# Attention with latent keys and values: the value and output weights on fp16 high/low parts with scales worked out on the chip, in place of float32r

## The reference

```python
xn = layernorm(x)
q = (xn @ wq)                 # 16 heads of 128 + 64 (rotary) columns
kva = xn @ wkv_a              # 128 latent + 64 rotary columns
ckv = rmsnorm(kva[:128]) * kv_norm_scale
kv = ckv @ wkv_b              # per head: 128 key columns, 128 value columns
scores = (q_nope . k_nope + rope(q_pe) . rope(k_pe)) * 192 ** -0.5
attn = softmax(causal(scores))
out = concat_heads(attn @ v) @ wo          # wo: 16 * 128 rows, 512 columns
ffn = sum over r of (xn @ factors[r]) / sqrt(8) + bias
return x + out + ffn
```

## Time and profile before

| | |
|---|---|
| median of 3 runs | 1571.4 us (1571.31 to 1575.96) |
| profiled execution | 1576.8 us, span of its trace 1574.7 us |
| busy in the span: TensorE, VectorE, ScalarE, GpSimd | 96%, 66%, 60%, 58% |
| TensorE instructions | 7876 |
| mean granted TensorE clock | 0.988 of full |
| the chain that ended last | TensorE 86%, VectorE 6%, ScalarE 4% |

### The profile page before, as it was taken

One profiled execution on the slowest core, in us unless ns is written; L12 is line 12 of the kernel. 1 busy time (PEld: TensorE's weight loads), 2 busy tenths in 40 slices (PEclk: granted clock), 3 DMA queues, 4 the chain that ended last, 5 costly groups with the idle time before them and its releaser, 6 DMA issues.

```text
span 1574.7 us, 25255 instructions
## 1 busy us (share of the span) xinstructions
PE 1514.0 (96%) x7876; PEld 819.7 (52%) x7876; DVE 1033.9 (66%) x2356; ACT 952.3 (60%) x2329; POOL 915.3 (58%) x897
## 2 busy tenths in 40 slices
PE   5669999999999999999999999999999999999998
PEld 4524555555555555455555555555555555555555
DVE  6755667666766665555555555556756776786887
ACT  6654766676666756556666666665546566554554
POOL 2665666566666666556656565656636655564553
PEclk9879999999999999999999999999999999999999
DMA  8635787878777789678777677787867667864564
GB/s 268 213 91 114 154 166 147 162 159 164 166 158 160 145 167 192 137 155 182 151 171 147 141 155 153 159 170 145 192 135 148 145 148 158 183 145 111 131 146 131
DMA packets 646883, 246.68 MB, mean 157 GB/s; under 512 B 599392, under 2 KB 612192, under 8 KB 646112
## 3 DMA queue, kind: packets, MB, share of 16 engines
q1 hardware_dynamic: 646752, 245.08, 72.3%
HBM read 79.30 MB, written 23.07 MB: 65 GB/s over the span
## 4 chain that ended last, share of the span: by engine, by line
PE 86%; DVE 6%; ACT 4%; issue 2%; POOL 1%; DMA 0%; SPq 0%; ACTq 0%; DVEq 0%; POOLq 0%
PE ps L356 17%; PE ps L358 17%; PE ps L357 17%; PE ps L491 7%; PE ps L496 7%; PE ps L497 7%; PE ps L492 7%; PE ps L493 7%; ACT ex L701 2%; DVE gm L1017 1%; DVE ps L1019 1%; DVE kt L966 1%; DVE acc L1062 0%; DVE nm L1035 0%; DVE stats L813 0%
## 5 line engine op out<-in xcount | busy, mean ns | idle before, releaser
L1218 POOL TENSOR_TENSOR st<-ex,st 128x512 f16<-128x512 f32 (+3 forms) x640 | 636.7, 1012 | 552.0 <-ACT st L711 540.6
L701 ACT ACTIVATE ex<-ps,nm,scales 128x512 f32<-128x512 f32 (+3 forms) x640 | 452.1, 709 | 542.5 <-DVE nm L1035 542.5
L1017 DVE TENSOR_REDUCE gm<-ps 128x1 f32<-128x512 f32 (+1 forms) x384 | 252.0, 669 | 209.7 <-PE ps L497 205.8
L711 ACT ACTIVATE st<-ex 128x512 f16<-128x512 f32 (+3 forms) x640 | 342.2, 561 | 6.1 <-ACT ex L701 0.4
L491 PE MATMUL ps<-kTh,q 128*128 128x512 f16 (+3 forms) x640 | 225.1, 352 | 5.5 <-DVE kRl L981 3.6
L496 PE MATMUL ps<-kRh,q 128*128 128x512 f16 (+3 forms) x640 | 223.4, 349 | 3.1 <-POOL q L1209 3.1
L492 PE MATMUL ps<-kTl,q 128*128 128x512 f16 (+3 forms) x640 | 223.8, 350 | 0.0
L493 PE MATMUL ps<-kTh,q 128*128 128x512 f16 (+3 forms) x640 | 223.7, 350 | 0.0
L497 PE MATMUL ps<-kRl,q 128*128 128x512 f16 (+3 forms) x640 | 223.4, 349 | 0.0
L356 PE MATMUL ps<-pT,vH 128*128 128x512 f16 (+3 forms) x640 | 223.2, 349 | 0.0
L357 PE MATMUL ps<-pT,vH 128*128 128x512 f16 (+3 forms) x640 | 222.2, 347 | 0.0
(11 more groups left out here) (187 smaller groups left out, 2282.7 us busy)
## 6 DMA issues: line engine op xcount, KB each, us to landing
wV<-w_vo SPq DMA_DIRECT2D x48, 512.0 KB, 3.7
wA<-w_abs SPq DMA_DIRECT2D x48, 256.0 KB, 3.0
pT<-st SPq DMA_TRANSPOSE x640, 3.2
early<-factors_in SPq DMA_DIRECT2D x32, 256.0 KB, 3.8
w_vo<-wV SPq DMA_DIRECT2D x16, 512.0 KB, 3.1
wP<-w_pe SPq DMA_DIRECT2D x24, 256.0 KB, 3.0
wsq<-wq_in SPq DMA_DIRECT2D x16, 256.0 KB, 3.5
wso<-wo_in SPq DMA_DIRECT2D x16, 256.0 KB, 2.9
```

What stands on the lines that cost most here:

```text
L701: e.activation(ex[:, n % NEX, 0:keys], s_bank(n)[:, 0:keys], ACT.Exp, bias=nm[:, (i * QT + r) % 4:(i * QT + r) % 4 + 1], scale=scales[:, p ...
L711: e.activation(stage(n, keys)[:, :, 0, :], ex[:, n % NEX, 0:keys].rearrange("p (t n) -> p t n", n=P), ACT.Copy).then_inc(z["a_pH"], 1)
L1017: e.tensor_reduce(m, b, AX_X, ALU.max).then_inc(z["v_max"], 1)
L1218: e.tensor_tensor(s[:, :, 1, :], ex[:, n % NEX, 0:keys].rearrange("p (t n) -> p t n", n=P), s[:, :, 0, :], ALU.subtract).then_inc(z["g_pL" ...
```

## The change

- `wX`, `wKV`, `wV` and `oT` become fp16 high and low parts. `wV` has a third slot, its high part divided by 2048, and the low part of `oT` is kept times 2048 (`LOW`), so the head output is three matmuls written out.
- Every head's value and output weight gets a scale: ScalarE squares and sums `wo` (`sqo`, 128x512, at r = 3) and the value weight (`sqv`, 128x128, at r = 0), TensorE sums both over the partitions ("nv", a 128x2 product with ones at r = 0), VectorE makes the scales (`scale_value`). 1/scale goes into `rden`.
- `w_o` moves from r = 0 to r = 1 (high part on ScalarE with the scale, low part from GpSimd to VectorE); "tkv" moves from r = 0 to r = 1, behind "tq"; "den" moves from r = 1 to r = 3 in the stage of chunk 3 and gets one more instruction everywhere.
- `read_output` gets one more ScalarE instruction, `oS` = high part times 2048, between the high part and VectorE's low part.
- In the prologue the transposes move from tiles 5 and 9 to 8 and 11, w_abs from 8 and 11 to 10 and 13. Storing and loading `w_vo` moves 384 KB in place of 512 KB.

```diff
@@ fills(i, r)
     if r == 0:
...
         if 1 <= i <= H:
-            out += [("wo", i - 1), ("wo_low", i - 1)]
+            out.append(("sqv", i - 1))
...
     if r == 0:
-        if i + 2 <= H + 2:
-            out.append(("tkv", i + 2))
+        if 1 <= i <= H:
+            out.append(("nv", i - 1))
...
         if i + 2 < H:
             out.append(("tq", i + 2))
-        if 1 <= i <= NU:
+        if i + 2 <= H + 2:
+            out.append(("tkv", i + 2))
+        if 1 <= i <= H:
+            out += [("wo", i - 1), ("wo_low", i - 1)]
+        if H <= i <= NU:
             out.append(("den", i - 1))
...
     if r == 3:
+        if 1 <= i < H:
+            out.append(("den", i - 1))
+        if 1 <= i <= H:
+            out.append(("ws", i - 1))
+        if i < H:
+            out.append(("sqo", i))
@@ buffers
-        wX = sb("wX", [P, 2, E], F32R)
-        wKV = sb("wKV", [P, 2, 2 * P], F32R)
+        wX = sb("wX", [P, 2, E], F16)
+        wKV = sb("wKV", [P, 2, 2 * P], F16)
-        wV = sb("wV", [P, 2, 2, E], F32R)
-        oT = sb("oT", [P, 2, CH], F32R)
+        wV = sb("wV", [P, 2, 3, E], F16)
+        oT = sb("oT", [P, 2, CH], F16)
@@ TensorE, head_output
+                    e.wait_ge(z["a_ws"], i + 1)
...
-                three(b, [oT[:, a, t * P:(t + 1) * P] for a in range(2)],
-                      [wV[:, i % 2, a, :] for a in range(2)]).then_inc(z["p_out"], 1)
+                o = [oT[:, a, t * P:(t + 1) * P] for a in range(2)]
+                e.matmul(b, o[0], wV[:, i % 2, 0, :], start=True, stop=False)
+                e.matmul(b, o[0], wV[:, i % 2, 1, :], start=False, stop=False)
+                e.matmul(b, o[1], wV[:, i % 2, 2, :], start=False, stop=True).then_inc(z["p_out"], 1)
+                elif kind == "nv":
+                    norm((kind, n), ("a_sqv", "a_sqo"), nv[:, :])
@@ ScalarE
+            def value_squares(kind, h):
...
+                e.activation(sqs[:, at:at + n], w, ACT.Square, accum_out=nv[:, at0:at0 + 1]).then_inc(
+                    z["a_" + kind], 1)
+
+            def w_vo_small(h):
+                e.wait_ge(z["v_wvo_hi"], h + 1)
+                e.activation(wV[:, h % 2, 2, :], wV[:, h % 2, 0, :], ACT.Copy, scale=1.0 / LOW).then_inc(z["a_ws"], 1)
@@ ScalarE, read_output
-                e.activation(oT[:, 0, :], ps[:, OB, :], ACT.Copy).then_inc(z["a_o"], 1)
+                e.activation(oT[:, 0, :], ps[:, OB, :], ACT.Copy, scale=shrink(chunk(i))).then_inc(z["a_o"], 1)
+                e.wait_ge(z["a_o"], i + 1)
+                e.activation(oS[:, :], oT[:, 0, :], ACT.Copy, scale=LOW).then_inc(z["a_oS"], 1)
@@ ScalarE, between the third and the fourth piece
-                                if kind in ("q", "wo", "parts"):
+                                if kind in ("q", "wo", "parts", "sqv"):
@@ VectorE
+            def scale_value(h):
...
+                e.wait_ge(z["p_nv"], h + 1)
+                e.tensor_tensor(t[:, 0:2], bank(("nv", h))[:, 0:2], tiny[:, :].broadcast_to([P, 2]), ALU.max).then_inc(
+                    z["v_nv"], 1)
+                e.wait_ge(z["v_nv"], h + 1)
+                root(t[:, 2:4], t[:, 0:2]).then_inc(z["v_vroot"], 1)
+                e.wait_ge(z["v_vroot"], h + 1)
+                e.tensor_tensor(t[:, 4:5], t[:, 2:3], t[:, 3:4], ALU.mult)
+                e.tensor_scalar(sc[:, 0:2], t[:, 2:4], WS, None, ALU.mult).then_inc(z["v_vw"], 1)
+                e.wait_ge(z["v_vw"], h + 1)
+                e.reciprocal(sc[:, 2:3], t[:, 4:5]).then_inc(z["v_vsc"], 1)
@@ VectorE, den
-                e.reciprocal(rden[:, i % 2, :], tsum[:, i % 2, :]).then_inc(z["v_den"], 1)
+                e.reciprocal(rtmp[:, i % 2, :], tsum[:, i % 2, :]).then_inc(z["v_rd"], 1)
+                e.wait_ge(z["v_rd"], i + 1)
+                if i < H:
+                    e.wait_ge(z["v_vsc"], i + 1)
+                e.scalar_tensor_tensor(out=rden[:, i % 2, :], in0=rtmp[:, i % 2, :], scalar=1.0 / (WS * shrink(c)),
+                                       in1=vsc[:, i % H, 2:3].broadcast_to([P, QT]), op0=ALU.mult,
+                                       op1=ALU.mult).then_inc(z["v_den"], 1)
@@ VectorE, read_output
-                e.wait_ge(z["a_o"], i + 1)
-                e.tensor_tensor(oT[:, 1, :], ps[:, OB, :], f(oT[:, 0, :]), ALU.subtract).then_inc(z["v_o"], 1)
+                e.wait_ge(z["a_oS"], i + 1)
+                e.scalar_tensor_tensor(out=oT[:, 1, :], in0=ps[:, OB, :], scalar=LOW * shrink(chunk(i)), in1=oS[:, :],
+                                       op0=ALU.mult, op1=ALU.subtract).then_inc(z["v_o"], 1)
```

More of the change, by code:

```diff
@@ L152, in fills @@
     return out
-IN_BANKS = ("q", "pe", "tkv", "wvo", "tq", "wabs", "out", "ffn", "nrm", "nf")
+IN_BANKS = ("q", "pe", "tkv", "wvo", "tq", "wabs", "out", "ffn", "nrm", "nf", "nv")
 def bank_order():
@@ L567, in _ @@
                 if t in (8, 11):
-                    w_abs(t // 3 - 2)
+                    wq_transpose(t // 3 - 2)
+                    kv_transpose(t // 3 - 2)
+                if t in (10, 13):
+                    w_abs(t // 3 - 3)
                 if t % 2 == 1 and 0 <= p - 2 < NP:
@@ L735, in fill @@
                     squares(kind, n)
+                elif kind in ("sqo", "sqv"):
+                    value_squares(kind, n)
+                elif kind == "ws":
+                    w_vo_small(n)
                 elif kind == "sqf":
@@ L803, in _ @@
                     for kind, n in fills(i, r):
-                        if last < 2 or r >= 2 or kind not in ("q", "wo", "parts"):
+                        if last < 2 or r >= 2 or kind not in ("q", "wo", "parts", "sqv"):
                             fill(kind, n)
@@ L900, in wq_transpose @@
                     e.wait_ge(z["p_wabs"], h)
-                e.tensor_copy(wX[:, 0, :], b).then_inc(z["v_tq_hi"], 1)
+                e.wait_ge(z["v_w2"], h // 2 + 1)
+                size = scales[:, h // 2, 0:1]
+                e.tensor_scalar(wX[:, 0, :], b, size, None, ALU.mult).then_inc(z["v_tq_hi"], 1)
                 e.wait_ge(z["v_tq_hi"], h + 1)
-                e.tensor_tensor(wX[:, 1, :], b, f(wX[:, 0, :]), ALU.subtract).then_inc(z["v_tq"], 1)
+                e.scalar_tensor_tensor(out=wX[:, 1, :], in0=b, scalar=size, in1=wX[:, 0, :], op0=ALU.mult,
+                                       op1=ALU.subtract).then_inc(z["v_tq"], 1)
             def kv_transpose(m):
-                cols = kv_cols(m)
-                b = bank(("tkv", m))[:, cols]
+                b = bank(("tkv", m))
+                parts = []
+                if m < H:
+                    e.wait_ge(z["v_w2"], m // 2 + 1)
+                    parts.append((slice(0, P), scales[:, m // 2, 1:2]))
+                if m >= 3:
+                    e.wait_ge(z["v_vw"], m - 2)
+                    parts.append((slice(P, 2 * P), vsc[:, m - 3, 0:1]))
                 e.wait_ge(z["p_tkv"], m + 1)
@@ L912, in kv_transpose @@
                     e.wait_ge(z["p_wvo"], m - 3)
-                e.tensor_copy(wKV[:, 0, cols], b).then_inc(z["v_tkv_hi"], 1)
+                for cols, size in parts:
+                    ins = e.tensor_scalar(wKV[:, 0, cols], b[:, cols], size, None, ALU.mult)
+                ins.then_inc(z["v_tkv_hi"], 1)
                 e.wait_ge(z["v_tkv_hi"], m + 1)
-                e.tensor_tensor(wKV[:, 1, cols], b, f(wKV[:, 0, cols]), ALU.subtract).then_inc(z["v_tkv"], 1)
+                for cols, size in parts:
+                    ins = e.scalar_tensor_tensor(out=wKV[:, 1, cols], in0=b[:, cols], scalar=size,
+                                                 in1=wKV[:, 0, cols], op0=ALU.mult, op1=ALU.subtract)
+                ins.then_inc(z["v_tkv"], 1)
             def w_abs(h):
@@ L1089, in fill @@
                     scale_pair(n)
+                elif kind == "nv":
+                    scale_value(n)
+                elif kind == "wo_low":
+                    w_o(n)
                 elif kind == "nf":
@@ L1249, in _ @@
                             scale_values(n)
-                        elif kind == "wo_low":
-                            w_o(n)
                         elif kind == "pe":
```

101 lines of the change are left out of this document (59 added, 42 removed).

## The result

The changed kernel takes 1630.1 us (median of 4 runs, 1627.1 to 1633.6), the kernel before 1571.6: 1.037 times as long, with an interval of 1.034 to 1.040. The forecast was 1627, in a range of 1596 to 1652.

What follows compares the result with a forecast made beforehand. TensorE was taken to bound chunks 3 to 1, a chain ScalarE, VectorE, TensorE chunk 0. Chunk 3's terms gave +54 us, the later stages and end +1.7; +55.7 on the median of 1571.4 made 1627, range 1596 to 1652.

Steps and rivals of the forecast that it cites:

- What bounds the kernel: TensorE decides in chunks 3 to 1, its waits paid in full; in chunk 0 a chain ScalarE, VectorE, TensorE.
- The wait of "nv": Chunk 3, r = 0: TensorE waits for sqv, queued behind q and exponentials on ScalarE; 42 us in sum.
- The clock: TensorE falls to 1.2 GHz behind long waits: nine of 2.5 us and more cost 15.3, those of 2.16 cost 5.
- "tkv" at r = 1: Even units: TensorE waits for the head output's bank, which VectorE reads; 0.7 us six times, 4 (bounds 0 to 15).
- The old waits before "nrm": TensorE's waits of 0.3 us in seven units go: minus 2.1 us.
- The cheaper matmuls: fp16 gains 0.08 us per head output, 20 over 256 if all count; w_abs and w_vo gain 9.5 in chunk 3.
- Chunks 2 and 1: Chunk 2: minus 4.8 us from matmuls; chunk 1: minus 1.8, as oS costs 3.0 there.
- Chunk 0: oS paid at 0.47 us in each of 16 heads, 7.6; den's instruction set against cheaper matmuls (bounds minus 4.8, plus 16).
- A: Rival: the waits come but the clock stays, or chunk 0 gains its matmuls in full; 1607 or 1592 us; chance 0.22.
- B: Rival: VectorE blocked by GpSimd at two-SBUF-input instructions in chunks 0 and 1; plus 15 to 20, 1645 us; chance 0.15.
- C: Rival: faster, "nv" finds its sums ready or TensorE's order does not bind; minus 28, 1543 us; chance 0.05.
- D: Rival: no change, waits of half the size and no clock effect nearly eaten by the gains; chance 0.03.

Runs made afterwards that it cites:

- Experiment 2: The changed kernel with 9 to 14 matmuls of 512 columns, their result overwritten, put on TensorE ahead of "nv"; 1615.6 us (1.026).
- experiment 1: The changed kernel with ScalarE's sqv ahead of the first exponential of r = 0 in place of behind q; 1604.9 us (1.021).
- experiment 4: The kernel before with only the fp16 high and low parts and fixed powers of two as scales, nothing moved; 1549.4 us (0.985).
- experiment 8: The kernel before with fp16 parts and fixed scales, plus oS as a copy on which VectorE's low part waits; 1558.5 us (0.991).
- experiment 9: The kernel before with fp16 parts and fixed scales, plus den's added instruction with a factor of one; 1551.5 us (0.987).
- experiment 6: The changed kernel with sqv ahead of the first exponential of r = 0 and "tkv" at r = 2, ahead of the values; 1598.6 us (1.017).
- experiment 7: The changed kernel with sqv ahead of r = 0's exponentials, "tkv" at r = 2, without oS, ws and wV's third slot; 1588.3 us (1.009).

## Why the prediction was right

**What bounds the kernel: right.** Waits in the stage of chunk 3 were paid in full. The stage lost 48.5 us where the sum had 54; of the 54, 5 belong to unit 1 (its wait 3.2, its product 0.2, its fall of the clock 1.7), which lies ahead of the cut, so like against like it is 49. That agreement is closer than its terms: the matmuls gained 11.1 there, not 13.7, and the clock took 16.2 more than before, not 18.6. The difference between the change and the types alone there, 562.5 - 502.9 = 59.5 us, is the sum of what the two profiles show: TensorE idle 42.7 against 5.6 (37.1), 84 against 8 slow matmuls (76 x 0.213 = 16.2), 15 products "nv" of 0.22 (3.3), and 0.165 for each of 15 more waits, because a printed wait begins at the end of a 0.38 us row while the next matmul would have started 0.215 behind its start (2.5). Together 59.1.

**The wait of "nv": right in place and size.** Forecast 42 us in sum; measured 42.5. Odd units 1.97 (2.16 forecast), even 3.15 (3.25; the first of them, unit 2, 3.62), units 1, 14 and 16 3.01, 2.53 and 3.25 (3.2, 2.6, 3.45). Three errors in single terms: `sqo` takes 0.61, not the 0.78 of an exponential of its size; 0.47, 0.47 and 0.78 are 1.72, not 1.74; and unit 15 was forecast with 0.3 on top of its old wait for q of 2.42, where "nv" took that wait's place with 2.53, so that the new waits net of the old one are 40, not 42.

**The clock: right in sum, by chance in its parts.** Forecast 20.3 us (15.3 and 5); 84 slow matmuls cost 17.9, of which 1.7 were there before. The rule "2.5 us and more falls, below half" did not hold unit by unit: the waits of 3.01 in unit 1 and 3.15 in unit 8 brought no fall, two of the six of 1.97 did, and the sum came near because these misses nearly cancel. Rows of the windows behind the wait in unit 4, in unit 8 and in unit 7, of 3.15, 3.15 and 1.97 us:

```profile
263.00:269.00 6.00, 5.40 (x20) 2.38 (x21) 3.64 (x11) 2.17 (x9) 2.50 (x3) 0.72 0.73 142
416.00:422.00 6.00, 5.42 (x31) 3.12 (x31) 5.36 (x17) 2.34 (x9) 2.10 (x3) 1.00 0.75 150
379.00:385.00 6.00, 6.00 (x25) 2.64 (x25) 3.11 (x10) 0.94 (x4) 1.67 (x3) 0.72 0.88 170
```

A fall cost 1.7 us (8 slow matmuls) in seven of its ten places, as the earlier trace rows had it. Experiment 2 shows that it is the standing still, and not the later start, that costs it.

**"tkv" at r = 1: right.** Forecast 0.7 in six units (4), measured 0.49 (2.9). The upper bound of 2.5, "if VectorE stayed as far behind", is what nearly came (2.36) when experiment 1 took the earlier wait away. The old waits before "nrm" (2.1 us) went, as forecast.

**The cheaper matmuls: right in kind, too large.** A head output gains 0.067 us in chunk 2 (4.26 over 64), not 0.08: the earlier trace rows are one place of 256, and the size was not checked against a second. By experiment 4 the types give 22 us, where the sum had 20 and 9.5.

**Chunks 2 and 1: -3.2 and -3.5 for -4.8 and -1.8.** The sum is right, the split is not. By experiment 8 oS costs 1.1 in chunk 2, 0.7 of it in one wait at its last heads; in chunk 1 the change is 0.8 over the types alone, where the forecast had 3.0 for oS: the slack of 0.1 in the earlier trace rows is that of one head.

**Chunk 0: right in sum, partly by chance.** Forecast +7.6, measured +9.0. That the chain through ScalarE pays for oS was right, its size was not: 0.47 in each of 16 heads was forecast, and what shows is 0.67 in each of nine waits, about one for a pair of heads, 6.0 by experiment 8. den costs 1.5 and the matmuls gain 2.7, which the sum had set equal. The falls of the clock, 2.8, were not in the sum for this stage, and 1.4 is without a cause.

**The rivals.** A (the clock stays) falls with the 84 slow matmuls and experiment 2. B (VectorE blocked by GpSimd at den, 15 to 20 us) falls with experiment 9, where den's instruction costs 1.5 us, all in chunk 0. Its rows in the changed kernel, and those of w_o's low part:

```profile
L1026 DVE SCALAR_TENSOR_TENSOR wV<-wso,vsc,wV 128x512 f16<-128x512 f32 x16 | 15.0, 935 | 15.6 <-ACT wV L711 15.6
L1136 DVE SCALAR_TENSOR_TENSOR rden<-rtmp,vsc 128x4 f32<-128x4 f32 x64 | 11.0, 173 | 2.2
```

den's new instruction takes 173 ns on average, with one of 0.53 us as the longest, and the low part of w_o 935 against the 751 of its neighbour in the earlier trace rows. The Trainium skill, page "SBUF — State Buffer", section "Who interferes with whom", lets a VectorE instruction with two SBUF inputs wait for a whole one of GpSimd that reads SBUF; these two lines neither need nor exclude it, and no run here has GpSimd idle beside them. C needed sqv ahead of the exponentials, which is experiment 1: the waits for it go, and yet it takes 1605 us and not 1543. D (waits of half the size, no effect of the clock) falls with the 42.5 us and the 84 slow matmuls.

## What to carry to other kernels

Where one engine has no idle time, price a new instruction on another engine by what stands ahead of it in that engine's queue, not by its own length: sqv is 0.3 us long, and TensorE waited 42.5 us for it in 16 units. Before moving the instruction away, look for the next lateness that its wait hides: here taking the wait away brought back 25 of the 60 us of waits and slow matmuls, because TensorE then waited for VectorE in other places. Keep what is cheap apart from what is not (a data type, and the machinery that feeds it), and time the first alone.

## What the runs showed that was not expected

- The clock's fall does not follow the length of a wait alone: 3.15 us without a fall in unit 8, 1.97 with one in unit 7, in the rows above; and the same wait for q, 3.16 us, has 7 slow matmuls behind it in experiment 6 and none in experiment 7. What decides it was not found.
- Filling a wait with matmuls whose result is thrown away made the profiled execution 21 us faster and the median 15, with no other change.
- The time up to head 0's copy differs between kernels by more than the change in it explains (175.7 us with the types alone, 186.0 in experiment 7); the clock granted from 60 to 120 us was 0.82 and 0.76 in these two. What sets it was not tried. The forecast left the start as it was; it is 0.4 us longer with unit 1's wait of 3.0 in it.
